# A state-space block and a mixture of experts: expert weights loaded in the routing stage, the next expert's rows turned between its predecessor's two layers, loops written out

## The reference

```
gates = softmax(h2 @ Wgate);  top 2 of 8 experts for each of the 4096 tokens
pos   = place of the token among those of its expert; kept if pos < capacity (1024)
exp_in[e, pos] = h2[token]                      # 8 experts x 1024 rows x 256
hmid  = gelu(exp_in[e] @ W1[e] + b1[e])         # 1024 x 1024
exp_out[e] = hmid @ W2[e] + b2[e]               # 1024 x 256
x     = x + sum over the token's two experts of gate * exp_out[e, pos]
```

## Time and profile before

| | |
|---|---|
| median of 3 runs | 4297.26 us (4292.94 to 4303.87) |
| profiled execution, its own time | 4288.75 us |
| its span on the core | 4287.2 us |
| PE, DVE, ACT, POOL busy | 3410.1, 2810.4, 2468.2, 1887.2 us |
| granted TensorE clock, mean of the span | 0.905 of full |

### The profile page before, as it was taken

One profiled execution on the slowest core, in us unless ns is written; L12 is line 12 of the kernel. 1 busy time (PEld: TensorE's weight loads), 2 busy tenths in 40 slices (PEclk: granted clock), 3 DMA queues, 4 the chain that ended last, 5 costly groups with the idle time before them and its releaser, 6 DMA issues. The chain is left out here.

```text
span 4287.2 us, 71027 instructions
## 1 busy us (share of the span) xinstructions
PE 3410.1 (80%) x22996; PEld 2126.2 (50%) x22996; DVE 2810.4 (66%) x4393; ACT 2468.2 (58%) x3862; POOL 1887.2 (44%) x1763
## 2 busy tenths in 40 slices
PE   8468788778787887885869999999999944699980
PEld 4146666666666666664534333333333324466660
DVE  4268888888888888885746777777777527101105
ACT  3268888888888888882221665566555631122110
POOL 0058888888888888884430010001000115100006
PEclk9679999999999999998986999999999976799995
DMA  5543333333333333335532001101010024222205
GB/s 201 154 109 90 90 90 90 90 90 90 90 90 90 90 90 90 92 88 226 213 108 92 6 22 19 19 6 21 19 19 6 11 86 149 76 76 81 81 22 193
DMA packets 160617, 360.57 MB, mean 84 GB/s; under 512 B 21475, under 2 KB 67542, under 8 KB 145808
## 3 DMA queue, kind: packets, MB, share of 16 engines
q1 hardware_dynamic: 127984, 269.57, 22.4%
q0 software_dynamic: 16784, 52.10, 3.4%
q10 hardware_dynamic: 15504, 34.61, 2.1%
HBM read 256.39 MB, written 102.26 MB: 84 GB/s over the span
## 5 line engine op out<-in xcount | busy, mean ns | idle before, releaser
L506 POOL TENSOR_TENSOR scan_hC<-scan_hh,scan_cbc 128x512 f32<-128x512 f32 x1024 | 1379.2, 1372 | 161.1 <-DVE scan_hh L718 104.3
L718 DVE TENSOR_TENSOR_SCAN scan_hh<-scan_dA,scan_state,scan_bx 128x512 f32<-128x512 f32 x1024 | 1253.2, 1265 | 212.0 <-PE scan_bx L810 103.1
L810 PE MATMUL scan_bx<-kept_ident,scan_dBxT 128*128 128x128 f32 x4096 | 678.9, 292 | 197.4 <-DVE scan_hh L718 134.9
L1557 PE MATMUL attend_s<-attend_kt,attend_qt 32*128 32x512 f32 (+3 forms) x2560 | 796.6, 611 | 34.0 <-DMA attend_qt<-attend_zero 27.6
L559 ACT ACTIVATE scan_dBxT<-scan_dtxT,scan_bt 128x512 f32<-128x512 f32 x1028 | 655.6, 710 | 81.9 <-PE scan_bx L810 81.7
L820 PE MATMUL scan_acc<-kept_ident,scan_hC 128*128 128x128 f32 x4128 | 657.9, 287 | 53.9 <-ACT scan_uu L568 28.4
L810 PEld LDWEIGHTS scan_bx<-kept_ident,scan_dBxT 128*128 128x128 f32 x4096 | 504.0, 150 | 389.4 <-DVE scan_hh L718 234.7
L554 ACT ACTIVATE scan_dA<-scan_dt,scan_an 128x512 f32<-128x512 f32 x1028 | 660.9, 712 | 29.0 <-DVE scan_hh L718 29.0
L1578 PE MATMUL attend_s<-attend_qt,attend_kt 32*128 32x512 f32 (+3 forms) x2560 | 637.9, 583 | 17.2 <-POOL attend_pb L1434 14.4
L1468 DVE TENSOR_REDUCE attend_mx<-attend_s 128x1 f32<-128x512 f32 x768 | 494.5, 686 | 197.3 <-PE attend_s L1557 196.1
L820 PEld LDWEIGHTS scan_acc<-kept_ident,scan_hC 128*128 128x128 f32 x4128 | 518.4, 150 | 68.8 <-POOL scan_hC L506 36.9
(11 more groups left out here) (202 smaller groups left out, 3904.3 us busy)
## 6 DMA issues: line engine op xcount, KB each, us to landing
scan_xs<-scratch_xin SPq DMA_DIRECT2D x288, 256.0 KB, 6.2
scan_cbc<-scratch_crows SPq DMA_DIRECT2D x64, 1024.0 KB, 4.7
scratch_y<-scan_uu ACTq DMA_DIRECT2D x17, 1024.0 KB, 4.2
route_at<-scratch_attn SPq DMA_DIRECT2D x160, 64.0 KB
scratch_xin<-proj_out_x SPq DMA_DIRECT2D x8, 1024.0 KB, 6.0
scratch_sz<-proj_out_z SPq DMA_DIRECT2D x8, 1024.0 KB, 6.4
scratch_exp_in<-proj_cleared SPq DMA_DIRECT2D x8, 1024.0 KB, 8.3
mix_yf<-scratch_y SPq DMA_DIRECT2D x8, 1024.0 KB, 6.7
```

Source lines behind the costliest of these rows:

```text
L506: pool.tensor_tensor(hC[n % 2][:, m, :], h[:, m, :], rows, ALU.mult).then_inc(hc_ok, 1)
L718: dve.tensor_tensor_scan(hh[n % 2][:, m, r], dA[n % 2][:, m, r], bx[bank(j)][:, r], state[:, d, n, m:m + 1], ALU.mult, ALU.add).then_inc(h ...
L810: last = pe.transpose(bx[bank(j)][:, t * P:(t + 1) * P], dBxT[turned_slot(n)][:, t, m * P:(m + 1) * P], k["ident"][:, :])
L1557: pe.matmul(s1[v % S1][:, 0:w], qt[n % SETS][rows, t * P:(t + 1) * P], kt_[n % SETS][rows, c * C:c * C + w], start=True, stop=True).then_i ...
```

## The change

Three things change. The experts' weight buffers and their semaphores move into a stage "weights" that encloses routing and experts; the weights of expert 0 are issued on the sync queue in routing behind the loads of chunk 3, those of expert 1 behind chunk 5, and x has a semaphore of its own. TensorE turns the rows of expert e+1 between the two layers of expert e, and VectorE copies them before it takes out e's second layer. The loop over experts on every engine, and the loop over chunks on the sync queue in routing, are written out.

```diff
-            chunks(sp, load)
+            for t in range(B * NC):
+                load(t // NC, t % NC, t, t % 2, 0, 0)
+                if t in (3, 5):
+                    load_weights(sp, (t - 3) // 2)
...
+def load_expert_weights(sp, ew, e, w1, b1, w2, b2):
+    i = e % 2
+    loaded = ew["loaded"][i]
+    sp.dma_start(ew["w1t"][i][:, :, :], w1[e].rearrange("(k p) f -> p k f", p=P)).then_inc(loaded, 16)
+    sp.dma_start(ew["b1t"][i][:, :], b1[e].rearrange("p f -> p f")).then_inc(loaded, 16)
+    sp.dma_start(ew["w2t"][i][:, :, :], w2[e].rearrange("(f p) d -> p f d", p=P)).then_inc(loaded, 16)
+    sp.dma_start(ew["b2t"][i][:, :], b2[e:e + 1, :].broadcast_to([P, D])).then_inc(loaded, 16)
...
         def _(sp):
-            experts(sp, load)
+            for e in range(E):
+                if e >= 2:
+                    sp.wait_ge(turned, (e - 1) * NT)
+                    sp.wait_ge(y_ok, (e - 1) * ST)
+                sp.dma_start(xt[e % 2][:, :, :], xv[e]).then_inc(loaded_x[e % 2], 16)
+                if e >= 2:
+                    load_expert_weights(sp, ew, e, w1, b1, w2, b2)
...
+            def copy_turned(e):
+                if e:
                     dve.wait_ge(h_mm, e * NH)
+                for q in range(NT):
+                    dve.wait_ge(turned, e * NT + q + 1)
                     m, ch = q // CH, q % CH
                     dve.tensor_copy(xT[:, m, ch * C:(ch + 1) * C], turn[q][:, :]).then_inc(x_out, 1)
+            copy_turned(0)
+            for e in range(E):
+                if e + 1 < E:
+                    copy_turned(e + 1)
                 for j in range(ST):
...
+            turn_rows(0)
+            for e in range(E):
+                pe.wait_ge(loaded_w[e % 2], (e // 2 + 1) * 16 * NWEIGHTS)
+                pe.wait_ge(x_out, (e + 1) * NT)
                 for q in range(NH):
...
+                if e + 1 < E:
+                    turn_rows(e + 1)
                 for j in range(ST):
...
+        with Stage(nc, "weights") as held:
+            ew = expert_weights(nc, held)
+            route(nc, k, attn, xf, a["wproj"], a["g2"], a["b2ln"], a["wgate"], a["expert_iota"], x3, exp_in, slots,
+                  gates, lambda sp, e: load_expert_weights(sp, ew, e, a["w1"], a["b1"], a["w2"], a["b2"]))
+            run_experts(nc, k, ew, exp_in, a["w1"], a["b1"], a["w2"], a["b2"], exp_out)
```

More of the change, by code:

```diff
@@ L1625, in _, with route @@
             values(GROUPS * NSTEP - 1, 1)
-def route(nc, k, attn, xf, wproj, g2, b2, wgate, expert_iota, x3, exp_in, slots, gates):
+def route(nc, k, attn, xf, wproj, g2, b2, wgate, expert_iota, x3, exp_in, slots, gates, load_weights):
     with Stage(nc, "route") as s:
@@ L1952, in _, with expert_weights, run_experts @@
             chunks(pe, chunk)
-def run_experts(nc, k, exp_in, w1, b1, w2, b2, exp_out):
+def expert_weights(nc, s):
+    FT = FF // P
+    return {
+        "w1t": [s.sb(f"w1t{i}", [P, KD, FF]) for i in range(2)],
+        "w2t": [s.sb(f"w2t{i}", [P, FT, D]) for i in range(2)],
+        "b1t": [s.sb(f"b1t{i}", [P, FT]) for i in range(2)],
+        "b2t": [s.sb(f"b2t{i}", [P, D]) for i in range(2)],
+        "loaded": s.sems("loaded0", "loaded1"),
+    }
+NWEIGHTS = 4
+def load_expert_weights(sp, ew, e, w1, b1, w2, b2):
[5 more added lines that the diff above has]
+    sp.dma_start(ew["b2t"][i][:, :], b2[e:e + 1, :].broadcast_to([P, D])).then_inc(loaded, 16)
+def run_experts(nc, k, ew, exp_in, w1, b1, w2, b2, exp_out):
     ST = CAP // P
@@ L1961, in run_experts @@
     FT = FF // P
+    w1t, w2t, b1t, b2t, loaded_w = ew["w1t"], ew["w2t"], ew["b1t"], ew["b2t"], ew["loaded"]
     with Stage(nc, "experts") as s:
         xt = [s.sb(f"xt{i}", [P, ST, D]) for i in range(2)]
[L1964 to L1967, removed]
         xT = s.sb("xT", [P, KD, CAP])
@@ L1973, in run_experts @@
         py = [s.ps(f"py{i}", [P, D]) for i in range(2)]
-        loaded = s.sems("loaded0", "loaded1")
+        loaded_x = s.sems("loaded_x0", "loaded_x1")
         stored = s.pool_dma_sems("stored0", "stored1")
         (turned, x_out, h_mm, h_ok, y_mm, y_ok) = s.sems("turned", "x_out", "h_mm", "h_ok", "y_mm", "y_ok")
-        NL = 5
         xv = exp_in.rearrange("(e t p) d -> e p t d", e=E, p=P)
@@ L1981, in run_experts @@
         NH = CH * FT
[L1983 to L1986, removed]
+        NT = KD * CH
         @block.sync
         def _(sp):
[L1990 to L1998, removed]
-            experts(sp, load)
+            for e in range(E):
[5 more added lines that the diff above has]
+                    load_expert_weights(sp, ew, e, w1, b1, w2, b2)
         @block.gpsimd
         def _(pool):
-            def store(e, i, nth):
+            for e in range(E):
                 for ch in range(CH):
-                    pool.wait_ge(y_ok, (e + 1) * ST + (ch + 1) * JT)
+                    pool.wait_ge(y_ok, e * ST + (ch + 1) * JT)
                     hold(pool, k)
                     pool.dma_start(yv[e, ch], yt[ch][:, :, :]).then_inc(stored[ch], 16)
-            experts(pool, store)
             for ch in range(CH):
@@ L2015, in _ @@
         def _(dve):
[L2016 to L2020, removed]
+            def copy_turned(e):
+                if e:
                     dve.wait_ge(h_mm, e * NH)
+                for q in range(NT):
+                    dve.wait_ge(turned, e * NT + q + 1)
                     m, ch = q // CH, q % CH
                     dve.tensor_copy(xT[:, m, ch * C:(ch + 1) * C], turn[q][:, :]).then_inc(x_out, 1)
+            copy_turned(0)
+            for e in range(E):
+                if e + 1 < E:
+                    copy_turned(e + 1)
                 for j in range(ST):
-                    if j % JT == 0:
+                    if j % JT == 0 and e:
                         dve.wait_ge(stored[j // JT], e * 16)
                     dve.wait_ge(y_mm, e * ST + j + 1)
-                    dve.tensor_tensor(yt[j // JT][:, j % JT, :], py[j % 2][:, :], b2t[i][:, :], ALU.add
+                    dve.tensor_tensor(yt[j // JT][:, j % JT, :], py[j % 2][:, :], b2t[e % 2][:, :], ALU.add
                                       ).then_inc(y_ok, 1)
-            experts(dve, body)
         @block.scalar
         def _(act):
-            def body(e, i, nth):
-                act.wait_ge(loaded[i], nth * (16 * NL) + 16 * NL)
+            for e in range(E):
+                act.wait_ge(loaded_w[e % 2], (e // 2 + 1) * 16 * NWEIGHTS)
+                if e:
+                    act.wait_ge(y_mm, e * ST)
                 for q in range(NH):
@@ L2040, in body, with turn_rows @@
                     act.wait_ge(h_mm, e * NH + q + 1)
-                    act.wait_ge(y_mm, e * ST)
-                    act.activation(hid[ch][:, f, :], ph[q % 2][:, :], ACT.Gelu, bias=b1t[i][:, f:f + 1]
+                    act.activation(hid[ch][:, f, :], ph[q % 2][:, :], ACT.Gelu, bias=b1t[e % 2][:, f:f + 1]
                                    ).then_inc(h_ok, 1)
-            experts(act, body)
         @block.tensor
         def _(pe):
-            def body(e, i, nth):
-                pe.wait_ge(loaded[i], nth * (16 * NL) + 16 * NL)
-                for q in range(KD * CH):
+            def turn_rows(e):
+                pe.wait_ge(loaded_x[e % 2], (e // 2 + 1) * 16)
+                if e:
+                    pe.wait_ge(x_out, e * NT)
+                for q in range(NT):
                     m, ch = q // CH, q % CH
@@ L2055, in body @@
                         t = ch * JT + j
-                        last = pe.transpose(turn[q][:, j * P:(j + 1) * P], xt[i][:, t, m * P:(m + 1) * P],
+                        last = pe.transpose(turn[q][:, j * P:(j + 1) * P], xt[e % 2][:, t, m * P:(m + 1) * P],
                                             k["ident"][:, :])
                     last.then_inc(turned, 1)
-                pe.wait_ge(x_out, (e + 1) * (KD * CH))
+            turn_rows(0)
+            for e in range(E):
+                pe.wait_ge(loaded_w[e % 2], (e // 2 + 1) * 16 * NWEIGHTS)
+                pe.wait_ge(x_out, (e + 1) * NT)
                 for q in range(NH):
                     ch, f = q // FT, q % FT
-                    if q < 2:
-                        pe.wait_ge(h_ok, e * NH)
-                    else:
+                    if e * NH + q >= 2:
                         pe.wait_ge(h_ok, e * NH + q - 1)
                     for m in range(KD):
-                        last = pe.matmul(ph[q % 2][:, :], w1t[i][:, m, f * P:(f + 1) * P],
+                        last = pe.matmul(ph[q % 2][:, :], w1t[e % 2][:, m, f * P:(f + 1) * P],
                                          xT[:, m, ch * C:(ch + 1) * C], start=m == 0, stop=m == KD - 1)
                     last.then_inc(h_mm, 1)
+                if e + 1 < E:
+                    turn_rows(e + 1)
                 for j in range(ST):
@@ L2072, in body @@
                     pe.wait_ge(h_ok, e * NH + (ch + 1) * FT)
-                    pe.wait_ge(y_ok, (e + 1) * ST + j - 1)
+                    if e * ST + j >= 2:
```

(9 more changed lines are left out.)

## The result

The changed kernel takes 4272.87 us (median of 5 runs, 4271.88 to 4280.57) beside 4297.26 for the kernel before: ratio 0.9948, 95% interval 0.9937 to 0.9958, so 22 us (18 to 27) less. The forecast was 4278.7, 18.6 us less, in a range of 4267 to 4291.

What follows compares the result with a forecast made beforehand. TensorE was taken to set the pace in the experts, a chain of short steps in routing. Terms -7.0 - 10.1 - 2.1 - 1.8 + 2.0 + 0.4 = -18.6 us gave 4278.7 from the median 4297.26; range 4267 to 4291.

Steps and rivals of the forecast that it cites:

- x alone: Start of experts: first turning needs only expert 0's x, landing 5.4 us after issue; 7.0 us less.
- rival 2: Start of experts: x0 and x1 land together at 9.9 us, saving only 2.5; total 4283.2 us; chance 0.07.
- Turning between the layers: Experts: TensorE's 1.44 us wait for copies goes at 7 boundaries; 10.1 us less.
- rival 3: Experts: VectorE's copies or a late second layer give back the 10.1 us; total 4288.8 us; chance 0.06.
- Loops written out: Experts: three repeated ScalarE table loads go, 2.1 us less; routing: sync-queue loads issue faster, 1.8 us less.
- Weights in routing: Routing: each of two weight sets delays an x3 store by 1.0 us; 2.0 us more, bounds 0 to 13.
- Rival 1: Routing: both weight sets hold the x3 store 6.5 us each, 13.0 not 2.0; total 4289.7 us; chance 0.13.
- Stage more: After the experts: the weights stage's own clearing block, two clears and a barrier; 0.4 us more.
- Rival 4: Experts: some 10 new instruction packets from memory hold TensorE; total +12 us, up to some +30; chance 0.06.

Runs made afterwards that it cites:

- undo_turn: Changed kernel with the turning of the next expert's rows put back behind the second layer, copies behind that layer's outputs; 4287.5 us, ratio 0.9983.
- written_out_only: Kernel before with only its loops written out (experts, and the sync queue's chunks in routing); 4289.7 us, ratio 0.9988.
- both_at_3: Changed kernel with both experts' weight sets issued behind the loads of chunk 3; 4279.8 us in 1 run.
- late_weights: Changed kernel with both weight sets issued only behind the last x3 of routing; 4274.7 us, ratio 0.9948.
- spread_weights: Changed kernel with each weight set in two halves, one half behind the loads of each of chunks 2 to 5; 4273.4 us, ratio 0.9950.
- undo_early: Changed kernel with the weights of experts 0 and 1 loaded at the start of the experts again, x keeping its own semaphore; 4272.8 us, ratio 0.9947.
- late_warm24: late_weights plus 24 unread unit-matrix transposes on TensorE ahead of the first turning; 4264.5 us, ratio 0.9926.
- after_again: The changed kernel itself measured once more, for a second profile; 4274.2 us, ratio 0.9950.

## Why the prediction was right, and where its terms were off

**x alone**: -7.0 forecast; the wait went from 12.4 us to 6.0 and 5.4 in the two profiles, since x0 landed after 6.0 and 5.4 us with x1 behind it. Right, and rival 2 with it refuted.

**Turning between the layers**: -10.1 forecast; -11.3 by undo_turn, -10.7 by written_out_only (465.1) beside both_at_3 (454.4). The mechanism was right, the copies are hidden, and rival 3 did not come. The term was sized by the wait alone. Of its 1.44 us, 0.17 go with the loops; on the other side the turning passes in 1.75 us in place of 1.91, and 0.1 us a boundary remains unexplained.

**Loops written out**: -2.1 for table loads and -1.8 for issue. The layers of written_out_only gave -3.3, of which 3 x 0.69 = 2.1 are table loads; the rest is 0.17 us at each boundary, in the waits for the copies, which the forecast gave to the turning whole. Issue gave 1.4 to 1.9 in routing: the six kernels with this issue and no collision lie at 214.3 to 216.3 us, the two with the loop at 217.7 and 218.2.

**Weights in routing**: +2.0 forecast, some +3.5 measured by late_weights and spread_weights. The step that failed is the size: I let a set be over 7.2 us after the loads in front of it, and the store be held by two fifths of the 2.6 us that were left. In fact the set did not run at 311 GB/s from its issue on: it was issued at 3527.53, the engines moved 112 and 135 GB/s in the next two microseconds, then they were full from about 3529.5 to 3538.5, with the indirect sends among the traffic from 3534.5. The store stood for 3.0 us and landed after 7.9, where 4 to 5 were to show that the forecast was right; the store behind the second set landed after 4.9 and 4.5. Rival 1's mechanism was there, in about a quarter of its price of 13.0. The price bought little: with the weights loaded at the start of the experts again (undo_early) the stages are 1.4 us shorter than with the change. Where the weights meet no store that is waited for (late_weights, spread_weights) they are 3.3 to 3.9 us shorter: it was the place that cost the gain, not the loading ahead.

**Stage more**: +0.4 forecast; 0.2 by the column "to next". Ten clears in place of eight:

```profile
L73 POOLq EVENT_SEMAPHORE_RANGE_CLEAR  x10: 37/38/38, 4165.7 to 4166.6; - x10
```

**Not in the sum**: the clock. I left expert 0's turning and the start of its layer as they were. In both profiles of the changed kernel TensorE is still at half clock for the first 4 us of the layer: +1.8, since the layers take 456.2 us where they take 454.4 with the clock up, in late_warm24 and, without extra products, in both_at_3. x being earlier is not the reason by itself: in both_at_3 and undo_turn it is as early, and the clock was up.

**Rival 4**, instructions from memory: the page of the changed kernel has

```profile
q8 instruction: 189, 3.10, 0.3%
```

where before it had 179 packets. The ten new packets of the estimate are there, and TensorE has no idle time in the experts that they could have caused, bursts of loads included.

**The sum**: -6.7 - 11.3 - 2.7 - 1.6 + 3.5 + 0.2 + 1.8 = -16.8 us (-11.3 and -2.7, or -10.7 and -3.3, are the layers' total of -12.2 less the clock), as the stages show (709.9 and 710.6 to 693.4 and 693.1). Forecast were -18.6: terms of both signs were off and nearly met, so that the total lies nearer than its terms is luck.

**What stays open**: the ratios say -22 and -21.5 us, their intervals -15 to -28. -16.8 lies inside that of after_again and just outside that of the first measurement. The 4 to 5 us between are not seen in any profiled execution: what lies outside the four columns took 3577.3 and 3581.6 us before (span less sum), 3585.5 and 3578.6 after. written_out_only, undo_turn, late_weights and spread_weights agree with their stage sums within some 2 us; undo_early is 4 us past its own as well, late_warm24 more than 6. What most of this goes with can be read from the mean granted clock of each run. A straight line through the 51 runs of the kernel before that are listed with it falls by 2.8 us for each 0.001 of clock. At the same clock, the runs of the changed kernel lie 17.7 us under this line, those of after_again 19.2, undo_early 20.2 and late_warm24 23.4: all within some 2 us of their stages (an estimate of mine, with the clock listed to 0.001 only). So these kernels' few runs had a clock somewhat higher than those of the kernel before, 0.9062 and 0.9057 against 0.9047 on average for the first two. Whether that is chance is not settled.

## What to carry to other kernels

A wait for several transfers under one semaphore is as long as the last of them: giving the one that is needed first its own semaphore won the shorter wait here, and moving the others into an earlier stage won nothing more as long as they met a store on the path there; spread or late, they won some 2 us by the stages (689.5 and 689.8 against 692.0 in undo_early). Before moving a transfer forward, look for the store that somebody waits for on the other queue, and let the burst be over before it. Where an engine waits for copies of what it has just made, put work of the next piece in between, provided that the copies are shorter than that work.

## What the runs showed that was not expected

**A store can stand behind a burst on another queue.** It landed in 3 to 4.5 us without such a burst, in 7.9 and 8.0 (9.2 in undo_turn) with 2.2 MB issued 5 to 6 us before it on another queue, in 12.6 with 4.5 MB. For the first 3 to 5 us it moved not a byte. The Trainium skill, "DMA: Bandwidth & Descriptors", section "Queues, rings and completion order", has each DMA engine take turns between the queues packet by packet. The trace agrees for the second phase of both_at_3, in which bytes of both queues move side by side; in the first phase it shows no turns. What holds the store there is not shown.

**TensorE's clock does not come up at the same moment after the same work.** TensorE's granted clock before and after, in the window ahead of its rise and the one in which it rises (before, then after):

```profile
3699.00:3701.00 2.00, 2.00 (x10) 1.70 (x8) 1.75 (x3) 0.00 (x0) 0.00 (x0) 0.50 1.04 412
3701.00:3703.00 2.00, 1.14 (x4) 0.56 (x4) 0.69 (x1) 0.00 (x0) 0.00 (x0) 0.87 1.07 379
```

```profile
3705.30:3707.30 2.00, 2.00 (x3) 0.67 (x2) 0.00 (x0) 0.00 (x0) 0.00 (x0) 0.50 0.00 0
3707.30:3709.30 2.00, 2.00 (x5) 0.72 (x3) 0.00 (x0) 1.60 (x2) 0.00 (x0) 0.81 0.00 0
```

Within the second window of each pair it goes from half to full. So it rose some 4 us after the first turning began (3697.43) before, almost 9 us after it (3699.31) in the changed kernel and likewise in after_again, late_weights and spread_weights, and again after some 4 in undo_turn and both_at_3, whose work up to there is the same. That is 1.8 us of expert 0's first layer, 30.0 against 28.2. What decides is not shown. The idle time ahead of the turning does not order it: 21.9 and 22.1 us where it rose after 4 in undo_turn and both_at_3, 22.7 to 23.2 where it rose after 9, but 28.5 to 28.9 in the kernels with one semaphore for all loads, where it rose after 4 again.
